# Moving the SBUF buffers of a gated cross-attention and FFN kernel to other addresses

## The reference

```python
lilora_weight = up_aux @ (lora_up @ (lora_down @ down_aux))
def xattn(h, ctx):                       # scores, softmax over 77 context rows, mix
    p = softmax(einsum('bsd,bvd->bsv', h, ctx)); return einsum('bsv,bvd->bsd', p, ctx)
x = x + tanh(g_xattn) * xattn(layernorm(x), ctx)
x = x + tanh(g_ffn) * (layernorm(x) @ (W + lilora_weight).T + b)
```

## Time and profile before

| | us |
|---|---|
| median of 3 runs | 307.21 (306.92 to 309.72) |
| the profiled execution | 307.34 |
| span of the profiled execution, first to last instruction | 305.3 |
| outside the span (307.34 - 305.3) | 2.04 |
| TensorE busy in the span | 297.3 |

### The profile page before, as it was taken

The page is one execution under the profiler, slowest core; times in us unless marked ns, Lnnn a source line. Parts: engine busy times, 40 slices in busy tenths (PEclk is TensorE's granted clock), DMA queues, the critical chain, the costliest instruction groups (busy, mean ns, idle before and its releaser), DMA issues.

```text
span 305.3 us, 6504 instructions
## 1 busy us (share of the span) xinstructions
PE 297.3 (97%) x2072; PEld 284.6 (93%) x2072; DVE 230.3 (75%) x797; ACT 184.6 (60%) x540; POOL 224.4 (74%) x274
## 2 busy tenths in 40 slices
PE   7999999999999999999999999999999999999992
PEld 5799999999999999999999999999999999999992
DVE  2787778885887778787588778777877787778765
ACT  2775666563775666566475566556765675567552
POOL 3478877785687877787578877787778777887763
PEclk9999999999999999999999999999999999999998
DMA  7854665442785494455364588544445565444003
GB/s 207 323 181 149 241 208 207 160 174 84 253 274 203 160 251 182 151 207 208 107 193 177 194 258 276 213 172 146 165 160 187 208 208 206 170 154 161 32 39 137
DMA packets 16750, 56.39 MB, mean 185 GB/s; under 512 B 2118, under 2 KB 2134, under 8 KB 16717
## 3 DMA queue, kind: packets, MB, share of 16 engines
q1 hardware_dynamic: 16281, 55.19, 52.5%
q10 hardware_dynamic: 436, 0.80, 0.8%
HBM read 35.84 MB, written 16.78 MB: 172 GB/s over the span
## 4 chain that ended last, share of the span: by engine, by line
PE 95%; DMA 2%; DVE 1%; ACT 0%; ACTq 0%; POOLq 0%; issue 0%; POOL 0%; DVEq 0%
PE y_ps L601 68%; PE y_ps L655 10%; PE a_ps L650 10%; PE y_ps L632 2%; PE c_ps L591 2%; DMA low_out_sb<-in_low_out 2%; PE a_ps L608 1%; PE y_ps L619 0%; PE y_ps L700 0%; PE y_ps L704 0%; PE y_ps L708 0%; PE c_ps L582 0%; DVE o_sb L834 0%; ACT squares L501 0%; DVE x L796 0%; DVE up_st L884 0%
## 5 line engine op out<-in xcount | busy, mean ns | idle before, releaser
L601 PE MATMUL y_ps<-wc,xT 128*128 128x256 f32 x1524 | 226.2, 302 | 0.0
L601 PEld LDWEIGHTS y_ps<-wc,xT 128*128 128x128 f32 x1524 | 212.4, 189 | 2.0
L396 POOL TENSOR_TENSOR x_bias<-x,bias_g 128x512 f32<-128x512 f32 x63 | 81.6, 1295 | 60.4 <-DVE x L796 60.4
L384 POOL TENSOR_TENSOR xT<-xt_raw,xT 128x512 fp32r<-128x512 f32 x64 | 83.2, 1300 | 0.1
L487 ACT ACTIVATE expd<-y_ps,neg_max,rs 128x77 f32<-128x77 f32 x64 | 26.7, 417 | 82.0 <-DVE neg_max L783 82.0
L407 POOL TENSOR_TENSOR rs<-stat_eps,half_neg 128x2 f32<-128x2 f32 (+1 forms) x67 | 46.2, 689 | 5.2
L834 DVE SCALAR_TENSOR_TENSOR o_sb<-y_ps,rs,x_bias 128x512 f32<-128x512 f32 x64 | 47.5, 742 | 0.6 <-POOL rs L407 0.6
L501 ACT ACTIVATE squares<-x,x_nmean 128x512 f32<-128x512 f32 x64 | 45.4, 710 | 1.7 <-DVE x_nmean L804 1.7
L655 PEld LDWEIGHTS y_ps<-stacks,pT 110*128 110x128 f32 (+1 forms) x256 | 40.0, 191 | 5.9
L772 DVE BATCH_NORM_STATS2 bn<-x_sb 128x6 f32<-128x512 f32 x64 | 43.8, 685 | 0.0
L796 DVE SCALAR_TENSOR_TENSOR x<-a_ps,x_sb 128x512 f32<-128x512 f32 x64 | 43.7, 682 | 0.2 <-PE a_ps L650 0.2
(11 more groups left out here) (81 smaller groups left out, 191.8 us busy)
## 6 DMA issues: line engine op xcount, KB each, us to landing
x_sb<-in_x SPq DMA_DIRECT2D x32, 512.0 KB, 4.4
xt_raw<-in_xt SPq DMA_DIRECT2D x31, 512.0 KB, 5.3
out<-o_sb SPq DMA_DIRECT2D x31, 512.0 KB, 3.0
stacks<-v_hi SPq DMA_DIRECT2D x2, 308.0 KB
w_all<-in_w SPq DMA_DIRECT2D x2, 256.0 KB, 6.5
out<-o_sb SPq DMA_DIRECT2D x2, 256.0 KB, 2.0
stacks<-v_hi SPq DMA_DIRECT2D x2, 252.0 KB
stacks<-v_lo SPq DMA_DIRECT2D x2, 252.0 KB
```

The source lines that it names most:

```text
L384: pool.tensor_tensor(xT[:, k % TRING, 1, :, :], xt_raw[:, k % XRING // UNIT, k % UNIT, :, :], xT[:, k % TRING, 0, :, :].bitcast(F32), ALU. ...
L396: pool.tensor_tensor(x1_bias[:, q, :], x1[:, j, :], bias_g[:, :], ALU.add).then_inc(x1b_ready, 1)
L601: mm = pe.matmul(y_half(k, h)[:, 0:n], xT[:, k % TRING, part, c, :], wc[:, c, w, h * H:h * H + n], start=(c == 0 and part == 0 and w == 0) ...
```

## The change

Only the order of the declarations changes, and with it the addresses. No instruction, wait, transfer, shape or name is changed, and each engine's instructions stand in the same order with the same waits. (In the new file they stand three lines higher.) `w_part` is only a view of `w_all`.

```diff
         ident = sb("ident", [P, P])
+        wc = sb("wc", [P, KC, 2, D + VP], F32R)
+        x_sb = sb("x_sb", [P, XRING, D])
+        low_in_sb = sb("low_in_sb", [low_in.shape[0], LR + D])
+        low_out_sb = sb("low_out_sb", [U, LR + D])
+        v_hi = sb("v_hi", [P, 2 * D], F32R)
+        v_lo = sb("v_lo", [P, 2 * D], F32R)
+        stacks = sb("stacks", [P, 2, 2, 2 * D], F32R)
+        ct = sb("ct", [P, 2, 2, KC, P], F32R)
+        w_all = sb("w_all", [P, 2 + KC * D])
+        xT = sb("xT", [P, TRING, 2, KC, P], F32R)
+        pT = sb("pT", [P, 2, 2, P], F32R)
+        p_ext = sb("p_ext", [P, 2, 1 + 2 * V])
+        up_st = sb("up_st", [LR, D], F32R)
+        dn_st = sb("dn_st", [LR, D], F32R)
+        c_rows = sb("c_rows", [P, D])
+        c_cent = sb("c_cent", [P, D])
         b_row = sb("b_row", [P, D])
...
+        expd = sb("expd", [P, 2, Q + V - 1])
+        bias_g = sb("bias_g", [P, D])
+        x1 = sb("x1", [P, 2, D])
         x1_bias = sb("x1_bias", [P, 4, D])
         o_sb = sb("o_sb", [P, ORING, D])
+        squares = sb("squares", [P, 2, D])
+        xt_raw = sb("xt_raw", [P, XRING // UNIT, UNIT, KC, P])
```

More of the change, by code:

```diff
@@ L63, in build_kernel @@
         eps = sb("eps", [P, 2])
[L64 to L75, removed]
         c_bn = sb("c_bn", [P, 6])
         c_mv = sb("c_mv", [P, 2])
[L78 to L87, removed]
         bn = sb("bn", [P, 2, 6])
@@ L93, in build_kernel @@
         neg_max = sb("neg_max", [P, 2])
-        expd = sb("expd", [P, 2, Q + V - 1])
         e_sum = sb("e_sum", [P, 2])
         e_inv = sb("e_inv", [P, 2])
-        p_ext = sb("p_ext", [P, 2, 1 + 2 * V])
-        pT = sb("pT", [P, 2, 2, P], F32R)
-        x1 = sb("x1", [P, 2, D])
         x1_sum = sb("x1_sum", [P, 2])
         x1_nmean = sb("x1_nmean", [P, 2])
-        squares = sb("squares", [P, 2, D])
+        expd = sb("expd", [P, 2, Q + V - 1])
+        bias_g = sb("bias_g", [P, D])
+        x1 = sb("x1", [P, 2, D])
         x1_bias = sb("x1_bias", [P, 4, D])
         o_sb = sb("o_sb", [P, ORING, D])
+        squares = sb("squares", [P, 2, D])
+        xt_raw = sb("xt_raw", [P, XRING // UNIT, UNIT, KC, P])
+        w_part = w_all[:, 2:2 + KC * D].rearrange("p (c o i) -> p c o i", c=KC, o=KC)
         y_ps = ps("y_ps", [P, YRING, 2, D])
```

## The result

The kernel after takes 305.82 us in the median (305.34 to 308.62, 20 runs), the kernel before 307.22 (306.92 to 310.3, 20 runs). The ratio is 0.9955 with a 95% interval of 0.9937 to 0.9973: a small gain, 1.4 us, which the interval tells from none, and inside the 1% that was called no change.

The account below looks back on a forecast made before the run. TensorE's matmuls were taken to bound the kernel. All terms were 0, so 305.3 + 2.04 outside the span gave 307.3 us, 307.2 by the median; range 302.5 to 311.5 us.

Parts of the forecast that it names:

- the 1% that was called no change: Whole kernel: a measurement tells about 1%, 3 us, from no change; a time within 1% was given 0.74.
- What bounds the kernel: Whole kernel: TensorE, busy 297.3 of 305.3 us and 95% of the chain, waits for nobody from 16.58 us on.
- Other engines and DMA have no part in the excess: TensorE's columns cost about 12% over one cycle, 28 us; moving other engines' and DMA's buffers away was valued at 0.
- The silent stretch: 147.71 to 147.98 us, other engines and DMA idle: 0.464 ns a column, against 0.465 in a busy stretch.
- the second term: TensorE's own two reads: streamed `wc`, `stacks` and loaded `xT`, `pT` stay apart, so 0, bounds -10 and +8 us.
- the first rival: TensorE's two reads collide and the new places avoid it: 297 us, at the far end 279; chance 0.13.
- its evidence from line 608: Line 608, with loads of 78 columns instead of 128, goes at 0.449 ns a column; taken for the faster rival.
- The signs named in advance: Right if a tile's pieces again read 0.11, 2.10, 0.47 to 0.48, 0.49, 1.17 to 1.18 us.
- Each tile streams all of them alike: 0: `wc`'s eight slices, 2,360 bytes apart, begin at all offsets in 64 bytes that steps of 8 give, in either layout: 0.
- the dearest and the cheapest row: Line 655, 0.479 ns a column, and line 608, 0.449; all columns at one or other would be +8 or -10 us.
- the rivals: Colliding reads avoided, 297 us, 0.13; new neighbours collide, 315 us, 0.13; only hidden engines change, 307 us, within the forecast's 0.74.
- The rule on odd starts: VectorE streams starting on an odd 4-byte word pay 1.30 instead of 1.054 ns a column; here all starts even, 0.

Follow-up runs that it names:

- the sequence alone: No computation left: TensorE alone runs the kernel's 31 matmuls of a tile on zeros at the addresses of the kernel before; 4.343 us a tile.
- phase64: Kernel after with `wc` slices 2,560 bytes apart, `wc` and `stacks` padded to multiples of 256 bytes, `xT` and `pT` 64 beyond: 302.2 us, ratio 0.9819.
- a_shift32: Kernel after with 32 bytes of padding behind `ident`, ahead of `wc`: tile 4.332 us, ratio 0.9978 to the kernel before.

## Why the prediction was right, and where not

- **What bounds the kernel** was right: TensorE in all traces, and no new wait: in the trace after, it waits once, 1.6 us in the opening. 30 ns a tile are 1.9 us in 64 tiles; the chain shows 1.60 and the medians 1.4.
- **Other engines and DMA have no part in the excess** was right. The silent stretch had suggested it, though it set matmuls of 334 columns against mostly 256s; the sequence alone with its 4.343 us, and `x_sb` moved away without effect (4.350), show it. Their buffers' moves cost nothing and their durations stayed.
- **The step that failed** is the second term, "Tables that were apart are still apart", valued at 0. It measured -30 ns a tile, -1.6 us in the chain. I measured nearness in KiB, which the 14 groups at 120.0 ns show to be without meaning, and the evidence against the first rival (the tables' spread over 16 and 18 KiB) had the same flaw. That rival's mechanism, a price that depends on TensorE's load beside its stream, is real, though its evidence from line 608 was weak: alone, a stream of 512 columns costs 228 to 232 ns with 128 or 32 loaded columns. The signs named in advance say so too: the products of `stacks` read 0.46 and 0.48 us after, below the 0.47 to 0.48 and 0.49 that were to stay.
- **The slices of `wc`** were the near miss. "Each tile streams all of them alike: 0" looked at the stream's start alone. Against an `xT` that starts 32 bytes further on, as after the change, the same eight slices meet other phases.
- **The sizes** were bounded well by the dearest and the cheapest row, -10 and +8 us, although these rows differ in the length of their streams: the layouts of whole kernels lie between 4.262 and 4.354 us a tile, -5.4 us in the median and none slower in it beyond the noise. The change reached 1.4 of it. That it stayed within 1% was luck as much as reasoning: its addresses, chosen for regions, happened to come to phases worth 30 ns a tile and not to the 88 of phase64.
- **What the Trainium skill says.** On the other engines the rule drawn on (SBUF — State Buffer, Who interferes with whom) agrees with the runs: 4.350 us with and without `x_sb` in its place. The same section gives TensorE two independent read ports and has it wait for nobody; it doesn't speak of addresses. Measured is 120.0 against 113.4 ns for the same stream, by the place of the load beside it alone, so here the load does change what the stream beside it costs. To leave the rivals a chance because no row moved a table was right. The rule on odd starts was not put to a test: all starts are even words here, and the 1.30 ns that the prediction took is the page's figure for pairs of words on both sources, not for one contiguous stream.

What stays open: why 6% remain with few loaded columns, why the matmuls around one change its length, why 64 bytes are best and 192 in the sequence are not, and whether the phase alone decides, since tiles with equal addresses differ by 32 ns in a_shift32.

## What to carry to other kernels

In a kernel that float32r matmuls bound, take the time between the starts of matmuls, divide by the columns, and compare matmuls of one shape in a silent stretch and a busy one. If both cost the same and more than one column per cycle, the excess is likely to be TensorE's own, as it was here. Then give all slices that are streamed, and all that are loaded, a spacing of a multiple of 256 bytes, and try the offset between the two groups in steps of 32 bytes; here 64 was best and worth 1.8%. Which buffer lies in which region was worth nothing that these runs could show, and an effect this small is read from the length of a tile, since the opening alone differs by 3 us between the traces.

## What the runs showed of the hardware

- A float32r matmul of 128 loaded and 256 streamed columns takes 120.0 ns at any of 14 distances of whole KiB, from 1 to 128, between the starts of load and stream. At 64 KiB and 64 bytes it takes 113.4 ns, and with 64 or fewer loaded columns 113.3 ns. Streams of 334 and 512 columns (150 to 152 and 228 to 232 ns) don't depend on the number of loaded columns.
- With slices 2,560 bytes apart the sequence of a tile takes 4.260 us with the loaded tables 64 or 320 bytes off and 4.301 to 4.339 us at the other 14 offsets.
- Without any other work on the core, and on zeros, the sequence of a tile costs the same as in the full kernel, to 7 ns of 4,350.
- The column of the granted clock read 1.00 while four transposes took 0.85 instead of 0.44 us (the trace after, to 14.6 us).
